# Softmax attention with a smaller score buffer and a maxima ring of two double places

## What is computed

```python
qkv = jnp.einsum('bnhd,hde->bnhe', xh, W_qkv) + b_qkv
q, k, v = jnp.split(qkv, 3, axis=-1)
scores = jnp.einsum('bihd,bjhd->bhij', q, k) / scale
p = jax.nn.softmax(scores, axis=-1)
attn = jnp.einsum('bhij,bjhd->bihd', p, v)
```

## Time and profile before

| What | Value |
|---|---|
| median of 3 runs | 2017.81 us (2017.28 to 2020.37) |
| profiled execution | 2012.94 us |
| its span, first to last instruction | 2011.3 us |
| PE busy | 1676.9 us (83%) |
| DVE busy | 1100.2 us (55%) |
| ACT busy | 621.2 us (31%) |
| POOL busy | 362.9 us (18%) |
| 768 reductions to maxima (L510) | 494.6 us of DVE |
| 384 exps (L568) | 372.3 us of ACT |

### The profile page before, as it was taken

How to read it: one execution, slowest core, us unless ns; L and a number is a source line. 1 busy time by engine, 2 the same in 40 slices (tenths; PEclk the granted TensorE clock), 3 DMA queues, 4 the chain that set the end, 5 groups by cost and what they waited for, 6 DMA issues and landing times. The chain is left out here.

```text
span 2011.3 us, 27514 instructions
## 1 busy us (share of the span) xinstructions
PE 1676.9 (83%) x8344; PEld 925.8 (46%) x8345; DVE 1100.2 (55%) x2511; ACT 621.2 (31%) x852; POOL 362.9 (18%) x424
## 2 busy tenths in 40 slices
PE   5869998998999989229996899997941699999973
PEld 3512332332333318216664576767820476666642
DVE  5868997997999806503333455544650233333354
ACT  3403665665666772001210201111110121221210
POOL 5530000000000001151112201001127111111255
PEclk9857999998999998559998799997865799999986
DMA  2486222222222006011111100005002011111123
GB/s 76 135 141 220 32 33 32 32 32 32 32 32 33 1 18 174 12 63 39 43 39 56 26 9 16 0 0 155 8 26 78 26 36 51 55 51 51 49 81 94
DMA packets 85586, 106.55 MB, mean 53 GB/s; under 512 B 10366, under 2 KB 71426, under 8 KB 84482
## 3 DMA queue, kind: packets, MB, share of 16 engines
q1 hardware_dynamic: 73806, 82.14, 17.0%
q0 software_dynamic: 10752, 22.03, 3.7%
q10 hardware_dynamic: 960, 1.57, 0.4%
HBM read 61.58 MB, written 44.14 MB: 53 GB/s over the span
## 5 line engine op out<-in xcount | busy, mean ns | idle before, releaser
L510 DVE TENSOR_REDUCE sa_half_max<-psum 128x1 f32<-128x512 f32 x768 | 494.6, 688 | 62.7 <-PE psum L614 44.0
L568 ACT ACTIVATE sa_probs<-psum 128x1024 f32<-128x1024 f32 x384 | 372.3, 1022 | 166.5 <-PE psum L605 164.9
L614 PE MATMUL psum<-k_stack,q_stack 96*128 96x512 bf16 x768 | 285.5, 410 | 28.2 <-PEq L398 18.1
L605 PE MATMUL psum<-q_stack,k_stack 97*128 97x512 bf16 x768 | 231.1, 384 | 6.2 <-ACT sa_probs L568 5.4
L1327 PE MATMUL psum<-w_e_up_a,ex_xt 128*128 (+1 forms) x576 | 217.8, 522 | 0.0
L1191 ACT ACTIVATE ex_silu<-psum 128x384 f32<-128x384 f32 (+1 forms) x144 | 74.8, 521 | 443.1 <-PE psum L1327 338.4
L637 PE MATMUL psum<-sa_probs,sa_v_ext 128*32 128x512 f32 x1536 | 206.9, 611 | 0.6 <-ACT sa_probs L568 0.6
L614 PEld LDWEIGHTS psum<-k_stack,q_stack 96*128 96x128 bf16 x768 | 75.0, 98 | 283.4 <-issue 151.2
L1212 DVE TENSOR_TENSOR ex_g<-ex_silu,psum 128x384 f32<-128x384 f32 (+1 forms) x144 | 84.6, 591 | 198.2 <-PE psum L1327 167.1
L1343 PE MATMUL psum<-w_e_down,ex_g_t 128*128 (+1 forms) x944 | 176.7, 339 | 13.3 <-issue 13.0
L1343 PEld LDWEIGHTS psum<-w_e_down,ex_g_t 128*128 128x128 f32 x944 | 154.5, 193 | 58.8 <-issue 58.8
(11 more groups left out here) (210 smaller groups left out, 1963.0 us busy)
## 6 DMA issues: line engine op xcount, KB each, us to landing
ex_x<-x_rows SPq DMA_DIRECT2D x56, 192.0 KB
y_rows<-ex_y SPq DMA_DIRECT2D x56, 192.0 KB, 2.0
q_stack<-qk_parts SPq DMA_DIRECT2D x66, 128.0 KB
k_stack<-qk_parts SPq DMA_DIRECT2D x66, 128.0 KB
x_rows<-sa_zeros SPq DMA_DIRECT2D x1, 6912.0 KB
qk_parts<-ep_parts SPq DMA_DIRECT2D x16, 384.0 KB
x_rows<-sa_zeros SPq DMA_DIRECT2D x1, 3840.0 KB
qk_parts<-ep_parts SPq DMA_DIRECT2D x16, 192.0 KB
```

What stands on the lines that cost most here:

```text
L510: nc.vector.tensor_reduce(half_max[:, g, hd, qt, half:half + 1], slot, AX.X, ALU.max).then_inc(ring_free[r], 1)
L568: nc.scalar.activation(probs[:, st % 2, 2 * pair:2 * pair + 2, :], ps[:, 2 * pair:2 * pair + 2, :], ACT.Exp, scale=SCALE0).then_inc(exp_do ...
L605: last = nc.tensor.matmul(ps[:, hd, :], kst[:, g, hd, kt * P:(kt + 1) * P], qst[:, g, hd, half * HALF:(half + 1) * HALF], start=True, stop ...
L614: last = nc.tensor.matmul(ps[:, 4 + r, :], qst[0:SK, g, hd, qt * P:(qt + 1) * P], kst[0:SK, g, hd, half * 512:(half + 1) * 512], start=Tru ...
```

## The change

The score buffer shrinks to three banks of one head each, taken in turn across steps and groups. PE waits for each single exp, ACT makes four exps of 512 columns a step, and the scores run six heads ahead of the values (SCORES_AHEAD) where they ran four. The ring has two places of two banks. A "max" unit is now two heads: two matmuls into the two banks and one DVE reduction over both, 128 x 2 x 512 elements to 128 x 2. A group has 32 such units, two in each step. "rows" and "out" units take a whole place and use its first bank. `half_max` gets another layout, so that the two halves lie apart. The order within a step changes, and another one holds in the last step of a batch. The semaphores of scores and exps count through a batch instead of a group.

```diff
-        SLOTS = 3
-        OUT = 4 + SLOTS
+        SCORES = 3
+        SLOTS, WIDE = 2, 2
+        RING_AT = SCORES
+        OUT = RING_AT + SLOTS * WIDE
         STEPS = 2 * TB
+        HEADS_BATCH = NG * GH * STEPS
...
-        half_max = sb("half_max", [P, NG, GH, TB, 2])
+        half_max = sb("half_max", [P, NG, 2, GH, TB])
...
-            return [("max", g, k // (2 * TB), k // 2 % TB, k % 2) for k in range(first, last)]
-
-        UNITS = GH * TB * 2
+            return [("max", g, WIDE * (k // (2 * TB)), k // 2 % TB, k % 2) for k in range(first, last)]
+
+        UNITS = GH // WIDE * TB * 2
...
+        def score_bank(g, st, hd):
+
+            return (GH * (STEPS * g + st) + hd) % SCORES
...
-                        sp.wait_ge(scores_done[g], START + 2 * STEPS * (b + 1))
+                        sp.wait_ge(scores_done, START + HEADS_BATCH * b + GH * STEPS * (g + 1))
                         load_stacks(sp, s, b + 1, g)
...
-                    nc.vector.tensor_reduce(half_max[:, g, hd, qt, half:half + 1], slot, AX.X,
+                    nc.vector.tensor_reduce(half_max[:, g, half, hd:hd + WIDE, qt], ps[:, at:at + WIDE, :], AX.X,
                                             ALU.max).then_inc(ring_free[r], 1)
...
-                for pair in range(2):
-                    act.wait_ge(scores_done[g], START + 2 * STEPS * b + 2 * st + pair + 1)
+                for hd in range(GH):
+                    act.wait_ge(scores_done, START + HEADS_BATCH * b + GH * (STEPS * g + st) + hd + 1)
...
-                    nc.scalar.activation(probs[:, st % 2, 2 * pair:2 * pair + 2, :], ps[:, 2 * pair:2 * pair + 2, :],
-                                         ACT.Exp, scale=SCALE0).then_inc(exp_done[g], 1)
+                    nc.scalar.activation(probs[:, st % 2, hd, :], ps[:, score_bank(g, st, hd), :],
+                                         ACT.Exp, scale=SCALE0).then_inc(exp_done, 1)
...
+                if n >= SCORES or not first:
+
+                    pe.wait_ge(exp_done, START + HEADS_BATCH * b + n - SCORES + 1)
+                nc.tensor.matmul(ps[:, score_bank(g, st, hd), :], kst[:, g, hd, kt * P:(kt + 1) * P],
+                                 qst[:, g, hd, half * HALF:(half + 1) * HALF], start=True, stop=True
+                                 ).then_inc(scores_done, 1)
...
                 if kind == "max":
                     hd, qt, half = unit[2:]
-                    last = nc.tensor.matmul(ps[:, 4 + r, :], qst[0:SK, g, hd, qt * P:(qt + 1) * P],
-                                            kst[0:SK, g, hd, half * 512:(half + 1) * 512], start=True, stop=True)
+                    for i in range(WIDE):
+                        last = nc.tensor.matmul(ps[:, at + i, :], qst[0:SK, g, hd + i, qt * P:(qt + 1) * P],
+                                                kst[0:SK, g, hd + i, half * 512:(half + 1) * 512], start=True, stop=True)
...
-            ORDER = ("scores", "maxima", "scores", "maxima", "maxima", "outputs", "maxima")
+            SCORES_AHEAD = GH + 2
...
+            ORDER = ("score", "score", "outputs", "score", "maxima", "score", "maxima")
+            LAST_ORDER = ("score", "outputs", "score", "score", "maxima", "score", "maxima")
```

More of the change, by code:

```diff
@@ L388, in softmax_attention @@
         max_stored, max_loaded, v_ready = map(per_group, ("max_stored", "max_loaded", "v_ready"))
-        scores_done, exp_done, pv_done, max_done = map(per_group, ("scores_done", "exp_done", "pv_done", "max_done"))
+        pv_done, max_done = map(per_group, ("pv_done", "max_done"))
+        scores_done, exp_done = (new_sem("sa_" + n) for n in ("scores_done", "exp_done"))
         ring_full = [new_sem(f"sa_ring_full{r}") for r in range(SLOTS)]
@@ L557, in exps @@
             def exps(b, g, st):
[L558 to L560 removed]
+                for hd in range(GH):
+                    act.wait_ge(scores_done, START + HEADS_BATCH * b + GH * (STEPS * g + st) + hd + 1)
+                    if hd == 0:
                         if st >= 2:
@@ L594, in _, with scores @@
         def _(pe):
-            def scores(b, g, st, pair, follows):
+            def scores(b, n, first):
+                st, hd = n // GH, n % GH
+                g, st = st // STEPS, st % STEPS
                 half, kt = st // TB, st % TB
-                if pair == 0 and st == 0:
+                if hd == 0 and st == 0:
                     pe.wait_ge(loaded[g], START + 16 * LOADS * (b + 1))
                     pe.wait_ge(max_loaded[g], START + 16 * (b + 1))
[L601 to L606, removed]
-                last.then_inc(scores_done[g], 1)
+                if n >= SCORES or not first:
[3 more added lines that the diff above has]
+                                 ).then_inc(scores_done, 1)
             def produce(b, unit, r, k):
@@ L623, in produce @@
                     for i in range(IT):
-                        last = nc.tensor.transpose(ps[:, 4 + r, i * P:(i + 1) * P],
+                        last = nc.tensor.transpose(ps[:, at, i * P:(i + 1) * P],
                                                    out_t[:, half, i * P:(i + 1) * P], s.ident[:])
@@ L647, in _ @@
             pe.wait_ge(ones_row, START + 1)
-            for pair in range(2):
-                scores(0, 0, 0, pair, None)
-            ORDER = ("scores", "maxima", "scores", "maxima", "maxima", "outputs", "maxima")
+            SCORES_AHEAD = GH + 2
+            for n in range(SCORES_AHEAD):
+                scores(0, n, True)
+            ORDER = ("score", "score", "outputs", "score", "maxima", "score", "maxima")
+            LAST_ORDER = ("score", "outputs", "score", "score", "maxima", "score", "maxima")
             def sequence(b, last):
@@ L658, in sequence @@
                         split, tail = step_units(g, st, last)
-                        final = last and g == NG - 1 and st == STEPS - 1
-                        nb, ng, nst = (b, g, st + 1) if st + 1 < STEPS else (b + (g + 1) // NG, (g + 1) % NG, 0)
-                        pair, left = 0, list(split)
-                        for what in ORDER:
-                            if what == "scores":
-                                if not final:
-                                    scores(nb, ng, nst, pair, (g, 2 * STEPS * b + 2 * st))
-                                pair += 1
+                        ahead, left = GH * (STEPS * g + st) + SCORES_AHEAD, list(split)
+                        for what in LAST_ORDER if g == NG - 1 and st == STEPS - 1 else ORDER:
+                            if what == "score":
+                                if ahead < HEADS_BATCH:
+                                    scores(b, ahead, False)
+                                elif not last:
+                                    scores(b + 1, ahead - HEADS_BATCH, False)
+                                ahead += 1
                             elif what == "outputs":
```

11 lines of the change are left out of this document (7 added, 4 removed).

## The result

| Kernel | Median | Runs | Profiled execution |
|---|---|---|---|
| before | 2018.19 us | 4 (2017.28 to 2020.37) | 2012.94 us, span 2011.3 |
| after | 2071.07 us | 4 (2060.22 to 2077.06) | 2075.69 us, span 2074.0 |

The ratio is 1.0247 (1.0206 to 1.0288): slower by 2.5%, 52.9 us where about 30 were forecast, and above the range of 2036 to 2062 us. The profiled pair differs by 62.7 us, the medians by 52.9. What follows splits the profiled pair.

The account below looks back on a forecast made before the run. PE was taken to set the step, so steady steps stay unchanged. Terms 14.8 + 16.0 - 6.0 + 1.1 + 3.5 + 0.7 = +30.1 us, added to the median 2017.81, gave 2047.9 us; range 2036 to 2062.

Parts of the forecast that it names:

- what sets the step: Main loop of the attention stage: PE's own work sets the 2.84 us step, with no wait in it.
- what a steady step pays: Steady steps: no change, wide reduction 1.22 us, DVE idle about 0.45 us, three score banks not stalling PE.
- The rival in which DVE sets the step: Steady steps: two wide reductions shorten the step to 2.60 us, -41 us, 2007 in all; chance 0.05.
- The tails: Ends of steps with a third ring unit: 18 "out" +14.8 us, 10 "rows" +16.0 us, together 30.8.
- the rival of free places: Tails find their ring place free or PE's loss is made up: 30.8 drops out, 2017 us; chance 0.07.
- Batch boundaries: First two boundaries: DVE's code fetch ends 14.6 us after the stack loads begin; -3.0 us each, -6.0 in all.
- rival with a dearer boundary: First two boundaries: code fetch starts with the branch, DVE returns at 17.1 instead of 12.4; +9, 2057 us; chance 0.10.
- hidden, by 0.9 us: Next group's maxima rows, first read in step 14: 3.1 us allowed from their evacuation, back in time, no cost.
- The steps without maxima: Last 20 steps with scores and no maxima: 2.38 us each where about 2.17 before, +3.5 us.
- The third boundary: Batch boundary without a branch: 2.9 us over a steady step where 1.8 before, +1.1 us.
- the prelude: Before the main loop: 0.7 us saved, as much lost to later first pairs, later loop start; +0.7 us.

Follow-up runs that it names:

- experiment 1: Kernel after with the "rows" and "out" tail units moved ahead of their step's first pair of maxima: 2038.59 us, ratio 1.0093 to before.
- experiment 2: Kernel after with the ring as four places of one bank and narrow reductions again, scores unchanged: 2046.51 us, ratio 1.0128 to before.
- experiment 10: Kernel before with two of the four score matmuls of a step cut in two, PE's body 1027 instead of 930: 1952.94 us, ratio 1.0009.
- experiment 11: Kernel before with each exp of two banks made as four of 256 columns, ACT's body 481: 2020.12 us, ratio 1.0017.
- experiment 3: Kernel after with the three batches of the hardware loop written out, so no engine branches: 2048.74 us, ratio 1.0129 to before.

## Why the prediction was wrong

**Right: what sets the step, and what a steady step pays.** PE's own work is 2.84 us in both kernels, the wide reduction takes 1.22, DVE rests 0.48 (forecast 0.45), and three score banks don't stall PE in a steady step. The rival in which DVE sets the step is refuted: DVE had 41.0 us less to do and not one steady step got shorter.

**Right: the tails.** 30.8 us were forecast, 31.9 measured, 4.16 us an "out" step (4.1) and 4.91 a "rows" step (5.0). Experiments 1 and 2 took the wait away in two ways and the time went with it, so the rival of free places is refuted too.

**Wrong: "Batch boundaries".** This is the step that failed. It took -6.0 and the trace shows +11.4, an error of 17.4 us. With it put right the forecast would have been 2065; the rest is the next point. The forecast read DVE's 8.15 us rightly as a code fetch behind the stack loads, and then kept it as a fixed event of the boundary: DVE would come back 14.6 us after the loads begin. But the fetch depends on how much code an engine has between two branches, and the change altered that for all three. DVE's went from 305 recorded instructions to 193, and its fetch vanished. ACT's went from 193 to 449 and PE's from 930 to 1074, and each now has one. Three things make them dearer than DVE's:
- They don't lie beside each other. The scores now run six heads ahead in three banks, so PE, still in step 15, needs the first exp that ACT makes behind its branch. ACT's absence comes first; PE waits 8.48 us for that exp, ends its step 15, and only then branches into its own fetch. Before, the last scores of step 15 waited only for exps of step 15, and PE reached its branch (318.95 us) within 1.1 us of ACT's and DVE's. In experiments 10 and 11 a fetch of PE or ACT lies beside DVE's and costs next to nothing.
- PE had work in DVE's absence until the ring was full. It has none in ACT's, since scores, exps and values all wait.
- A small part is the clock. Both kernels come back at 0.50. By the starts at that clock (0.43 us from one matmul of 512 columns to the next instead of 0.22) I estimate the loss at 3.1 us a boundary after and 2.2 before.

The prediction's rival with a dearer boundary (a fetch that starts with the branch, 2057 us) put it on DVE as well, and no such absence is in the trace.

**Wrong: "hidden, by 0.9 us".** The maxima rows of the next group were to be back in time for step 14. They weren't: PE's timeline in one such step, and SP's,

```profile
221.98 1.06 PE L651 MATMUL psum<-sa_probs,sa_v_ext 128*32 128x512 f32 x8
223.81 0.39 PE L617 MATMUL psum<-q_stack,k_stack 97*128 97x512 bf16 x1 [0.77 <-DMA q_stack<-max_rows_dram]
```

```profile
219.17 0.33 SPq L461 DMA_DIRECT2D max_rows_dram<-sa_max_rows  x1
221.93 0.25 SPq L463 DMA_DIRECT2D q_stack<-max_rows_dram  x1
```

The load is issued 2.76 us after the store here, and 1.34 us after it at the first boundary (320.23 to 321.57). I had allowed 3.1 us from the evacuation until the load's bytes are there, from one pair of rows. Four of ten steps 14 wait, 2.1 us in all. The trace shows what sets these four apart: an instruction packet of 16 KB (q8) begins 0.12 to 0.48 us after each of their stores, and the load follows the store by 2.19 to 2.76 us; the other eight stores of the trace have no such packet, and their loads follow after 1.34 to 1.40. The 14 traces together have 168 of these stores. 34 have an instruction packet under way or beginning within 1.1 us, and of these 30 take 1.84 us or more; of the other 134 only three do. Two of the four packets, at 386.76 and 554.08 us, are part of the code that PE fetches anew in the second and third pass. So two of the four waits, too, go back to the size of PE's body. Three steps 13 take 4.48, 4.47 and 4.09 us instead of 2.84, another 4.5; three short steps give back 0.7. These three come from the clock: the windows behind the two waits of the "rows" tail show, where the steps are long,

```profile
316.00:319.00 3.00, 2.03 (x11) 0.59 (x7) 2.62 (x3) 1.46 (x3) 0.00 (x0) 1.00 0.00 0
319.00:322.00 3.00, 2.44 (x11) 0.43 (x11) 0.96 (x3) 1.09 (x2) 0.00 (x0) 0.72 0.03 8
322.00:325.00 3.00, 3.00 (x16) 1.06 (x16) 1.49 (x2) 1.63 (x3) 0.00 (x0) 0.71 0.01 3
```

a granted clock of 0.72 and 0.71, a mean over stretches at full and at half speed (2.4 and 1.2 GHz). PE had waited 0.76 and 0.77 us just before it fell. That makes +6.0 us in all. It also hangs on the tails' wait: in experiment 1, without the two waits, no step 13 or 14 is longer than 2.84.

**Small terms.** The steps without maxima take 2.40 (2.38 forecast), and the stretch cost 3.9 instead of 3.5, counted from its first score. The third boundary is +1.3 (+1.1). In the prelude the first 32 wide reductions take 37.69 us where 64 narrow ones took 38.36, the 0.7 saved that was forecast; the first step then takes 4.16 instead of 3.17, and start and first step together are +0.2 (+0.7).

The sum of the forecast's terms was +30.1. Put 11.4 for -6.0, add 6.0 for steps 13 and 14, 1.1 for the tails, 0.4 for the steps without maxima, 0.2 for the third boundary and take 0.5 for the prelude: 54.7, where the stage's measured cost is 54.6.

**What stays open.** What the limits are in bytes of code and why ACT's limit (between 313 and 449 recorded instructions) isn't DVE's (between 290 and 305): instructions that the profile doesn't record, waits and register work, may count. Why an instruction packet holds the maxima's store up by 1 us or so, though it moves in another queue. Whether the ring's two places or the length of the wide reduction cost the tails more. Why TensorE's clock fell after three of ten "rows" tails here, and after eight of ten in experiment 3.

## What to carry to other kernels

A ring is counted in places, not in banks: whoever groups two fills into one place must look for units that take a place of their own, and for the reduction that each of them then waits for. At a hardware loop, count each engine's instructions between two branches before and after a change; an engine that passes its limit is away for some us, and what that costs depends on whether it lies beside another engine's absence or in a chain with it. Where such a body runs only a few times, as three here, write the loop out (0.9905 of the time before, which also spares ACT's table load behind each branch) or keep bulk DMAs away from the branch (0.9941). And see whether an engine ahead of its own branch needs something that another makes only behind its branch: that puts the absences in a chain.

## What the runs showed of the hardware

- The first instruction after a loop's branch came 0.3 us later in engines with a small body. With a large one it came 2.5 to 3.0 us later with the stack loads out of the way, and some 6 to 9.5 us later while these loads ran, with a DMA share of 0.94 before and 1.07 after. PE's absences were 3.3 to 3.9 us in the kernels made from after and 6.7 to 7.5 us in experiment 10, where the loads were running.
- The step from none to all is sharp: DVE was away 0.34 us with 290 recorded instructions (experiment 2) and 8.36 with 305 (before), though these two kernels differ in more than that.
- PE with a body of 1074 or 1027 fetched 18 packets of 16 KB in the second and third pass of the loop, with 930 none.
- Of 34 stores of maxima rows with an instruction packet beside them, 30 were followed by their load only after 1.84 us or more; without a packet it was 1.34 to 1.40 in 131 of 134 cases.
- ACT ran its table load of 1.28 us again behind each branch of the loop, and not between the written-out batches.
- A reduction of 128 x 1024 from PSUM takes 1.221 us and one of 128 x 512 takes 0.691: one in place of two is 0.16 us shorter. An exp of 1024 columns takes 1.02 us, one of 512 takes 0.597.
- Waits of PE of 0.76 and 0.77 us, 0.3 us of work apart, stood ahead of a fall of the granted clock (to a mean of 0.72 over 3 us) in three places of ten; single waits of 0.67 us ("out" tails) stood ahead of none in the steps behind them.
